# Second attention: root steps of seven layer norms on GpSimd, their products in two slots, one reciprocal a slot

## The reference, cut to what matters

```python
def _layernorm(x, axis=-1, eps=1e-05):
    m = jnp.mean(x, axis=axis, keepdims=True)
    v = jnp.var(x, axis=axis, keepdims=True)
    return (x - m) / jnp.sqrt(v + eps)
...
x = _layernorm(x + _L0_attn_ref(...))
# _L0_xattn_ref(ctx_1024, x, ...): image_embeds = ctx_1024 (154 a batch), latents = x (512 a batch)
    x = layer_norm(image_embeds, ln1_g, ln1_b)
    l = layer_norm(latents, ln2_g, ln2_b)
    q = l @ Wq
    kv = jnp.concatenate([x, l], axis=1) @ Wkv        # 16 heads of 64
    w = softmax(q * scale @ (k * scale))
    out = (w @ v).reshape(B, S_lat, INNER) @ Wo
x = _layernorm(x + _L0_xattn_ref(ctx_1024, x, ...))
```

## Time and profile before

| | us |
|---|---|
| median of 3 runs | 1597.56 (1596.67 to 1597.82) |
| the profiled execution | 1596.03, its span 1594.2 |
| TensorE busy in the span | 1433.5 (90%) |
| VectorE busy | 1132.2 (71%) |
| ScalarE busy | 923.1 (58%) |
| GpSimd busy | 713.8 (45%) |

### The profile page before, as it was taken

The page is one execution under the profiler, slowest core; times in us unless marked ns, Lnnn a source line. Parts: engine busy times, 40 slices in busy tenths (PEclk is TensorE's granted clock), DMA queues, the critical chain, the costliest instruction groups (busy, mean ns, idle before and its releaser), DMA issues.

```text
span 1594.2 us, 45033 instructions
## 1 busy us (share of the span) xinstructions
PE 1433.5 (90%) x19640; PEld 811.7 (51%) x19640; DVE 1132.2 (71%) x2307; ACT 923.1 (58%) x1301; POOL 713.8 (45%) x750
## 2 busy tenths in 40 slices
PE   8888888899989899998988988989999999999996
PEld 4222223344444335343434544777887888875453
DVE  6778877898977885868727668576777766474654
ACT  2787776788867776887672433555455544441220
POOL 2124131576756665676670107467776666010000
PEclk9999999999999999999999999999999999989898
DMA  4000003333322341332301000000000002000000
GB/s 166 1 1 1 1 1 108 99 102 91 95 78 78 92 109 57 98 91 78 95 16 70 1 1 14 16 17 17 4 17 17 17 4 92 3 2 1 8 7 14
DMA packets 32421, 70.84 MB, mean 44 GB/s; under 512 B 5329, under 2 KB 7057, under 8 KB 31969
## 3 DMA queue, kind: packets, MB, share of 16 engines
q1 hardware_dynamic: 32224, 67.98, 14.7%
HBM read 47.45 MB, written 20.51 MB: 43 GB/s over the span
## 4 chain that ended last, share of the span: by engine, by line
PE 56%; DVE 17%; ACT 16%; issue 7%; POOL 4%; ACTq 0%; DVEq 0%; POOLq 0%
PE ps L160 54%; ACT b_X L988 4%; ACT a_E L470 3%; DVE b_mx L926 2%; POOL b_EL L1006 2%; ACT b_EH L169 2%; DVE a_MX L433 1%; POOL d_XI L1814 1%; ACT b_Hk L842 1%; PE ps L242 1%; POOL d_tmp L1811 1%; DVE X L234 1%; DVE b_rd L1099 1%; DVE st L172 1%; DVE b_Lq L172 1%
## 5 line engine op out<-in xcount | busy, mean ns | idle before, releaser
L1006 POOL TENSOR_TENSOR b_EL<-b_X,b_EH 128x1024 f16<-128x1024 f32 x160 | 341.6, 2135 | 189.1 <-ACT b_EH L169 188.9
L988 ACT ACTIVATE b_X<-ps 128x1024 f32<-128x1024 f32 x160 | 163.7, 1023 | 86.8 <-PE ps L160 86.6
L1811 POOL TENSOR_TENSOR d_tmp<-d_G,d_XI 128x31 f32<-128x31 f32 (+15 forms) x248 | 127.7, 515 | 157.4 <-DVE d_G L1740 138.6
L433 DVE TENSOR_REDUCE a_MX<-ps 128x2 f16<-128x1024 f32 x128 | 155.1, 1227 | 44.7 <-PE ps L160 44.3
L169 ACT ACTIVATE b_EH<-b_X 128x1024 f16<-128x1024 f32 x160 | 169.1, 1057 | 27.0 <-PE ps L160 15.8
L160 PE MATMUL ps<-b_M,b_S 128*64 128x512 f16 (+1 forms) x1408 | 177.2, 384 | 3.3 <-ACT b_X L988 3.2
L926 DVE TENSOR_REDUCE b_mx<-ps 128x2 f32<-128x1024 f32 x128 | 155.7, 1217 | 28.8 <-PE ps L160 27.0
L470 ACT ACTIVATE a_E<-ps 128x1024 f32<-128x1024 f32 x128 | 131.3, 1026 | 49.5 <-PE ps L160 49.5
L1814 POOL TENSOR_TENSOR d_XI<-d_XI,d_tmp 128x31 f32<-128x31 f32 (+15 forms) x248 | 139.3, 562 | 19.4
L160 PEld LDWEIGHTS ps<-b_M,b_S 128*64 128x64 f16 (+1 forms) x1408 | 70.5, 109 | 83.9 <-ACT b_X L988 19.8
L452 POOL TENSOR_TENSOR a_QS<-a_QS,a_MR 128x512 f16<-128x512 f16 x16 | 18.5, 1157 | 183.6 <-ACT a_MR L169 179.7
(11 more groups left out here) (336 smaller groups left out, 3298.1 us busy)
## 6 DMA issues: line engine op xcount, KB each, us to landing
b_S<-s_xk SPq DMA_DIRECT2D x48, 336.0 KB, 6.4
b_M<-s_xq SPq DMA_DIRECT2D x48, 256.0 KB, 5.1
s_xk<-b_Hk SPq DMA_DIRECT2D x16, 336.0 KB, 2.2
s_xk<-b_Lk SPq DMA_DIRECT2D x16, 336.0 KB, 2.5
s_xq<-b_Hq SPq DMA_DIRECT2D x16, 256.0 KB, 2.0
s_xq<-b_Lq SPq DMA_DIRECT2D x16, 256.0 KB, 2.0
d_XI<-eye SPq DMA_DIRECT2D x8, 512.0 KB, 3.5
f_w<-f_w SPq DMA_DIRECT2D x1, 2048.0 KB, 8.6
```

The costliest lines, as they stand in the source:

```text
L433: v.e.tensor_reduce(out, PS[:, bk:bk + 2, :], AX, ALU.max).then_inc(sem("a_mx"), 1)
L988: a.e.activation(b_X[k % 2], PS[:, bk:bk + 2, :], ACT.Exp, scale=0.125).then_inc(sem("b_ex"), 1)
L1006: last = p.e.tensor_tensor(b_EL[k % 6], b_X[k % 2], b_EH[k % 6], ALU.subtract)
L1811: e.tensor_tensor(tm, a, x, ALU.mult).then_inc(*p.step())
```

## The change

- `b_norm_vector` and `b_norm_gpsimd` take the place of `normalize` for seven norms: keys 2 to 5 and the results of batches 0 to 2. VectorE keeps the statistics, variance + eps and the guess, both in one slot, and signals b_nx. GpSimd waits for it behind its low part and does ten small steps on 128x4, two behind each of five low parts (without the fused form, so ten for VectorE's seven), and signals b_ny. Seven slots after the guess VectorE makes the products, two in one slot and two in the next.
- The seven share the second set of st, bn and mv. GpSimd's start slots are written out: norm n begins on VectorE in slot 29, 42, 55, 87, 101, 131 or 175, and GpSimd's steps stand behind the low parts of slots three to seven on.
- The reciprocals of batches 0 to 2 are one a slot in four slots. So `B_OUT` is 27; TensorE's scalings, the output product, the add, the norm, the transposes of the result, and keys 5 come two slots later. The starts of the outputs (71, 115, 159) stay. The tail (batch 3) keeps its form.

```diff
+        def b_norm_vector(v, x, n, done, out):
+            e = v.e
+            x0, y = st[:, 4, :], st[:, 5, :]
+            for j in range(4):
+                last = e.bn_stats(bn[:, 1, j, :], x[:, j, :])
+                if j % 2:
+                    last.then_inc(*v.step())
+                    yield
+            v.wait_own()
+            for j in range(4):
+                last = e.bn_aggr(mv[:, 1, j, :], bn[:, 1, j, :])
+            last.then_inc(*v.step())
+            yield
+            v.wait_own()
+            e.tensor_scalar(x0, mv[:, 1, :, 1], 1.0, 1e-5, ALU.mult, ALU.add).then_inc(*v.step())
+            v.wait_own()
+            e.tensor_scalar(y.bitcast(I32), x0.bitcast(I32), -0.5, float(MAGIC), ALU.mult, ALU.add).then_inc(sem("b_nx"), 1)
+            for _ in range(7):
+                yield
+            v.wait_ge("b_ny", n + 1)
+            for j in range(4):
+                last = e.tensor_scalar(out[:, j, :], x[:, j, :], mv[:, 1, j, 0:1], y[:, j:j + 1], ALU.subtract, ALU.mult)
+                if j == 1:
+                    yield
+            last.then_inc(sem(done), 1)
+
+        def b_norm_gpsimd(p, n):
+            e = p.e
+            x0, y, a, b = st[:, 4, :], st[:, 5, :], st[:, 6, :], st[:, 7, :]
+            p.wait_ge("b_nx", n + 1)
+            e.tensor_tensor(a, y, y, ALU.mult).then_inc(*p.step())
+            p.wait_own()
+            e.tensor_tensor(b, a, x0, ALU.mult).then_inc(*p.step())
+            yield
...
+            p.wait_own()
+            e.tensor_scalar(b, b, -27.0 / 1024.0, 0.5625, ALU.mult, ALU.add).then_inc(*p.step())
+            p.wait_own()
+            e.tensor_tensor(y, y, b, ALU.mult).then_inc(sem("b_ny"), 1)
+            yield
...
-            if kind == "l":
+            if k > 1:
...
+                yield from b_norm_vector(v, x, k - 2 if k < 5 else 4, "b_ln", b_LX if kind == "l" else x)
...
-            for _ in range(4):
+            for _ in range(6 if b < NB - 1 else 4):
                 yield
...
                 e.reciprocal(b_rd[:, c], b_den[b % 2][:, c]).then_inc(*v.step())
-                if q % 2:
+                if q % 2 or b < NB - 1:
                     yield
...
-            yield from normalize(v, xb(b), 1e-5, "xr_B", fine=True)
-
-        B_OUT = 25
+            if b < NB - 1:
+                yield from b_norm_vector(v, xb(b), (3, 5, 6)[b], "xr_B", xb(b))
+            else:
+                yield from normalize(v, xb(b), 1e-5, "xr_B", fine=True)
+
+        B_OUT = 27
...
+        def b_side_gpsimd(p):
+            at = 22
+            for n, x in enumerate((29, 42, 55, 87, 101, 131, 175)):
+                yield from later(x + 3 - at, ())
+                yield from b_norm_gpsimd(p, n)
+                at = x + 8
...
+            side = b_side_gpsimd(p)
             for u in range(NU):
                 for s in range(11):
                     b_low_gpsimd(p, u, s)
+                    next(side, None)
```

More of the change, by code:

```diff
@@ L30 @@
     "f_bm": ("a_oc", 16), "f_xm": ("a_pv", 64),
-    "d_inv": ("a_ws", 4), "d_x1": ("b_kv", 6), "d_btm": ("b_kt", 6), "xr_E": ("xr_A", 4), "xr_F": ("xr_B", 4), "f_wh": ("d_wh", 3), "b_ws": ("ld_id", 16), "f_xb": ("a_xb", 4),
+    "d_inv": ("a_ws", 4), "d_x1": ("b_kv", 6), "d_btm": ("b_kt", 6), "xr_E": ("xr_A", 4), "xr_F": ("xr_B", 4), "f_wh": ("d_wh", 3), "b_ws": ("ld_id", 16), "f_xb": ("a_xb", 4), "b_nx": ("ld_cst", 16), "b_ny": ("ld_xt0", 16),
 }
@@ new lines, in b_norm_gpsimd @@
+        def b_norm_gpsimd(p, n):
[7 more added lines that the diff above has]
+            p.wait_own()
+            e.tensor_scalar(a, b, -10.0 / 3.0, None, ALU.add).then_inc(*p.step())
+            p.wait_own()
+            e.tensor_tensor(a, a, b, ALU.mult).then_inc(*p.step())
+            yield
+            p.wait_own()
+            e.tensor_scalar(a, a, 5.0, None, ALU.add).then_inc(*p.step())
+            p.wait_own()
+            e.tensor_tensor(y, y, a, ALU.mult).then_inc(*p.step())
+            yield
+            p.wait_own()
+            e.tensor_tensor(a, y, y, ALU.mult).then_inc(*p.step())
+            p.wait_own()
+            e.tensor_tensor(b, a, x0, ALU.mult).then_inc(*p.step())
+            yield
+            p.wait_own()
+            e.tensor_scalar(b, b, -27.0 / 1024.0, 0.5625, ALU.mult, ALU.add).then_inc(*p.step())
+            p.wait_own()
+            e.tensor_tensor(y, y, b, ALU.mult).then_inc(sem("b_ny"), 1)
+            yield
@@ L736, in b_keys_vector @@
             v.wait_ge("ld_cx", 32)
-            if kind == "l":
+            if k > 1:
+                x = xb(i) if kind == "l" else b_CX[:, 4 * i:4 * i + 4, :]
+                if kind == "l":
+                    v.wait_ge("xr_A", i + 1)
+                    v.wait_ge("b_kt", k)
+                yield from b_norm_vector(v, x, k - 2 if k < 5 else 4, "b_ln", b_LX if kind == "l" else x)
+            elif kind == "l":
                 v.wait_ge("xr_A", i + 1)
@@ L1256, in b_tail_scalar @@
         def b_tail_scalar(a):
-            yield from later(1 + B_OUT + 6, ())
+            yield from later(32, ())
             turn_scalar(a, "B", NB - 1)
```

## The result

The changed kernel ran in 1580.4 us (median of 5, 1576.6 to 1586.6), the kernel before in 1596.9 (median of 5): ratio 0.9923, 95% interval 0.9897 to 0.9949. It is faster than forecast, 1592.5 us with a range from 1586.5. The profiled execution, the fastest of the five, took 1576.58 us, its span 1574.8, 19.4 us less than before.

What follows compares the result with a forecast made beforehand. TensorE was taken as the bound; root steps 0.5, unit 14 -0.3, products 4.5, reciprocals 2.0, scaling -0.3 gave 6.4 us, less 1.4 for returning waits: 5 us, so 1592.5 us, range 1586.5 to 1599.

Steps and rivals of the forecast that it cites:

- What bounds the kernel: Second attention: TensorE is the bound, busy 39.56 of 43.41 us in one unit; only its idle time can be won.
- The step that failed: Scaling and output product two slots later: bank waits traded, net loss 0.3 us; transposes of batches and keys 5 cost 0.
- Products in two slots: Norms' last products: 0.35 us of TensorE wait a pair, 4.2 us against 8.67 us, gain 4.5 us.
- signs of being wrong: TensorE waiting for GpSimd's low parts before unit 14, a GpSimd step of 0.5 us or more, pairs over 2.2 us.
- rival C: Slower: in six norms' last two slots each pair of products waits for its own low part; 1604 us; chance 0.13.
- Root steps: Seven norms' small steps moved to GpSimd: almost none on the path, gain 0.5 us; a pair costs GpSimd 0.5 us.
- Unit 14: Seventh norm's ten GpSimd steps, nothing to spare, against the guess step no longer waiting 2.12 us: loss 0.3 us.
- Reciprocals and scaling: Reciprocals one a slot, gain 2.0 us; scaling and output product two slots later, net loss 0.3 us.
- The 1.4 us taken off: TensorE's waits for the projections' low parts partly come back when other waits go: 1.4 us off the 6.4 us sum.
- Rival A: Stalls at the maxima return as waits for projections' low parts, gain 0 to 3 us, about 1596 us; chance 0.29.
- Rival B: All the waits go because VectorE, free of root steps, arrives on time: 12 us, 1585.5 us; chance 0.12.

Runs made afterwards that it cites:

- e6_place: Kernel before, with only batch results' norms, their transposes and keys 5 begun two slots later (four products in slot 10): stretch of stage B 506.6 us against 514.4, ratio 0.9958.
- e2_split: Kernel before with only the last products split over two slots (7 and 8), root steps on VectorE: stretch of stage B 506.6 us against 514.4, ratio 0.9975.
- e7_outs_one_slot: Changed kernel, but the three batch results' norms make their four products in one slot (10): stretch of stage B 502.0 us against 504.0, ratio to before 0.9945.
- e1_recip: Kernel before with only reciprocals one a slot and the two slots' shift behind them; norms as before: stretch of stage B 507.6 us against 514.4, ratio 0.9979.
- e3_gps: Kernel before with only the root steps on GpSimd, four products in slot 8: stretch of stage B 519.6 us (514.5 estimated without clock falls), ratio 1.0047.
- e5_gps_split: Kernel before with root steps on GpSimd and products split over slots 7 and 8, reciprocals two a slot: stretch of stage B 506.5 us, ratio 0.9963.
- e9_best_dve: Changed kernel with batch results' and keys' products, reciprocals' casts and low parts in slots 10, root steps on VectorE: stretch 498.9 us (498.6 on GpSimd), ratio to before 0.9923.
- e4_split_recip: Changed kernel with only the root steps back on VectorE: stretch of stage B 506.8 us against 504.0, ratio to before 0.9948.

## Why the prediction was wrong

**What bounds the kernel** held: TensorE does, and the gain came out of its waits in stage B, most of all those behind the last products. The list of waits has one row more than I used: TensorE's weight loads (PEld) did wait for GpSimd's low parts, 3.9 us before and 3.0 after, at most 0.4 us at a time.

**The size of the whole.** I forecast 5 us; 10.4 us is the change and the remaining 6 us of the first comparison's 16.5 is the granted clock outside stage B, which no step of the prediction had. The 10.4 us alone, taken from the 1597.56 us that the forecast started from, would give 1587.2 us, just inside the range (from 1586.5). That the time fell 6 us below the range is the luck of the clock; that the change is worth twice the forecast is not. I had taken 3.2 us for what a measurement can tell; single executions of either kernel differ by 15 to 16 us.

**The step that failed** is the one that let everything move two slots later and booked 0.3 us of loss for it, with the transposes at 0. I priced that shift by banks alone. But GpSimd's low parts aren't alike from slot to slot: in slot 10 it is 1.16 us, with 2 us of nothing behind it. I had worked with a low part of 2.13 us in every slot of 2.8 us and an arrival at no particular time, 0.8 us a pair. Reading VectorE's slot against GpSimd's list, one slot after the other, would have shown that the products go from slot 8 into 9 and 10. e6_place shows what the shift is worth: it alone gives 7.8 us, 0.9 of them by the transposes of batch 2.

The same working mis-sized a second term, the split. e2_split, the split alone in the old slots, gives 7.8 us where I had 4.5. The two don't add up to 15.6 us: in units 7 and 11 both take away the same 2.43 us waits, and both shorten unit 14. So the 5.4 us by which the whole exceeds the forecast has no single owner. By the terms of the sum it is: products 6.2 us instead of 4.5, units 14 and 15 1.7 instead of -0.3, reciprocals and scaling 2.6 instead of 1.7, 1.4 us taken off and not needed, root steps nothing instead of 0.5.

**Products in two slots.** Forecast 4.5 us, waits of 8.67 us going to 4.2. In the full change units 7 and 11 gave 2.2 us each and the keys 1.8 us (what is left of units 1 to 5, 8 and 9 once the reciprocals' 0.86 us a batch is taken off), 6.2 us in all. The keys' part is the split's. Of units 7 and 11 it would be wrong to say so: in slots 9 and 10 the split is a loss there (e7_outs_one_slot). Gain and loss nearly cancel, and e1_recip, which has no split, would be at 504.0 us too but for unit 5. The pair that I bounded by 2.8 us took 3.16, since two GpSimd parts in a row each stopped one product. That was one of my signs of being wrong (over 2.2 us), and rightly: the mean arrival doesn't describe these pairs. It didn't decide for rival C, because the second pair cost nearly nothing.

**Root steps.** "Almost none of that is on the path" is shown: e3_gps (by the estimate at full clock), e5_gps_split and e9_best_dve are within 0.3 us of their counterparts. The exception is e4_split_recip, 2.9 us behind the changed kernel by one step in unit 5. Moved alone, with keys 4's and 5's products in one slot, the steps even went with two waits that were longer (2.76 and 2.77 us for 0.89). A small step took 0.20 us (0.22 for the form with a constant), a pair some 0.45 us from start to the next low part; I had 0.5. The guess step got through at once (0.17 us), and GpSimd waited 0.31 us for it in batch 0's norm. By the Trainium skill (Perfetto Trace Analysis, Optimizing Scalar/DVE Operations), moving work between these two might not help: the runs agree in three of these four pairs, since the work had been hidden.

**Unit 14.** I booked 0.3 us of loss for ten steps with nothing to spare; units 14 and 15 gave 1.67 us. In unit 14 TensorE's waits of 0.81 and 0.48 us for the maxima, behind the guess step of 2.12 us and the step after it (1.53 us), are gone. They are gone in every run, with the steps on either engine, so letting the guess step through did not need GpSimd's wait for it: e2_split has 26.99 us with it on VectorE. In unit 15 it is ScalarE's copy of batch 2's transposes that moved out of the way (e6_place). Nor is the products' place the reason: e3_gps, with all four where they were, lost both waits of unit 14 too (27.28 us), and e2_split has unit 15 as before.

**Reciprocals and scaling.** Forecast 2.0 - 0.3 = 1.7 us. Units 12 and 13, which have nothing else of the change, gave 1.36 - 0.50 = 0.86 us a batch, 2.6 us for three. The 0.69 us went as said. The new waits for the projections' low part at slot 7 came at 0.57 us, none at slot 8. Not foreseen were the 0.96 us behind the casts in slot 9 and the 1.27 us before keys 5's transposes, which had stood at 0.

**The 1.4 us taken off** for waits that come back wasn't needed: units 7 and 11 have 0.38 and 0.20 us for projections where they had 0.19 and 0.58. Rival A is refuted: stage B gained 10.4 us, and it allowed 3. Rival B (1585.5 us) was nearest in size; its reason, a punctual VectorE, is not the one.

Open in part is the wait of 2.38 us in unit 5 of e1_recip and e4_split_recip. The traces show who began first: GpSimd's low part there, by 0.02 to 0.03 us, and b_rp in both profiles of the changed kernel, by 0.14 us. They don't show why VectorE comes to it some 0.16 us later with the root steps on it; I did not vary that by itself.

## What to carry to other kernels

Where two engines stop each other, write the two lists side by side, slot by slot, before pricing a move: a piece of work costs by the slot that it stands in, and a shift that was only a by-product can be worth more than the parts that were meant. Put together what needs the other engine's silence in the slot where that engine is silent, rather than splitting it evenly. And compare a stage by its own stretch of the trace when the rest of the program swings with the clock.

## What the runs showed of the hardware that I had not expected

- TensorE's granted clock differs from one execution to the next of the same program: means of 0.972 to 0.986 for the kernel before, and 1599.3 to 1583.6 us with them. By the straight lines through the times of the two kernels, each us at the lower level cost 0.33 to 0.38 us.
- Five waits of TensorE, of 1.9 to 2.8 us, in a busy stage (one in e1_recip, three in e3_gps, one in e4_split_recip) had a fall of the clock beginning in them or within 2 us behind them, 1.7 us beside the wait itself by the estimate in e3_gps. Three waits of 2.43 us had none, two in the profile of the kernel before and one in e3_gps itself, at 671.6 us. So the length of the wait alone does not decide it.
- Two GpSimd instructions in a row let one VectorE instruction in between them: a pair of products of 0.33 us each took 3.16 us. The Trainium skill (SBUF — State Buffer, SBUF: two separate sides) has the pair held for a whole instruction by whoever starts first, which fits: 2.13 and 1.16 us of GpSimd's, one after the other. Who starts first can hang on a tenth of a us: b_rp, 0.48 us when it began 0.14 us ahead of a low part, took 2.38 us when it began 0.02 us behind one.
